# A graph network on one core: the prologue's work dealt out anew among VectorE, ScalarE and GpSimd

## What is computed

```python
def reference(x, adj, W1, b1, W2, b2, W):        # x 128x128x64, adj 128x128x128, about 12% of it > 0
    h = relu(layernorm(x))
    mask = (adj > 0)
    W1a, W1b = W1[:F], W1[F:]
    diff = h[:, :, None, :] - h[:, None, :, :]
    g = relu((h @ W1a)[:, :, None, :] + diff @ W1b + b1)
    x = x + einsum('bjkh,bjk->bjh', g, mask) @ W2 + mask.sum(-1)[..., None] * b2
    h = relu(layernorm(x))
    return x + einsum('bnm,bmf->bnf', adj, h) @ W.T
```

## Time and profile before

| | us |
|---|---|
| median of 3 runs | 849.71 |
| lowest, highest | 849.04, 850.85 |
| the profiled execution, its own time | 851.92 |
| its span in the trace | 849.9 |

### The profile page before, as it was taken

One profiled execution on the slowest core, in us unless ns is written; L12 is line 12 of the kernel. 1 busy time (PEld: TensorE's weight loads), 2 busy tenths in 40 slices (PEclk: granted clock), 3 DMA queues, 4 the chain that ended last, 5 costly groups with the idle time before them and its releaser, 6 DMA issues.

```text
span 849.9 us, 26682 instructions
## 1 busy us (share of the span) xinstructions
PE 809.7 (95%) x8242; PEld 712.0 (84%) x8243; DVE 820.1 (96%) x2908; ACT 794.5 (93%) x2241; POOL 610.8 (72%) x1164
## 2 busy tenths in 40 slices
PE   3779999999999999999999999999999999999996
PEld 1447888988898889888988898888888988998884
DVE  6989999999999999999999999999999999999994
ACT  4768999999999999999999999999999999999993
POOL 0855777777787777777777777777777777777773
PEclk9779999999999999999999999999999999999998
DMA  9800000000000000000000000000000000000000
GB/s 336 324 1 2 2 14 20 21 15 20 21 20 9 21 21 18 17 21 21 20 9 21 20 21 15 21 20 20 8 20 21 20 14 21 21 20 9 27 1 23
DMA packets 26704, 27.54 MB, mean 32 GB/s; under 512 B 3520, under 2 KB 24512, under 8 KB 25536
## 3 DMA queue, kind: packets, MB, share of 16 engines
q1 hardware_dynamic: 25488, 25.37, 8.8%
q10 hardware_dynamic: 1072, 0.43, 0.2%
HBM read 21.59 MB, written 4.19 MB: 30 GB/s over the span
## 4 chain that ended last, share of the span: by engine, by line
PE 84%; DVE 6%; issue 3%; ACT 3%; POOL 2%; DMA 1%; SPq 0%; ACTq 0%; POOLq 0%; DVEq 0%
PE ring L400 45%; PE ring L428 8%; PE prep L457 4%; DVE acc L804 4%; PE post L494 3%; PE post L500 3%; PE post L487 3%; PE post L488 3%; PE prep L465 3%; PE prep L468 2%; PE prep L463 2%; PE post L492 2%; POOL rstd L969 1%; DMA x_all<-x_nbf_dram 1%; PE prep L459 1%
## 5 line engine op out<-in xcount | busy, mean ns | idle before, releaser
L804 DVE SCALAR_TENSOR_TENSOR acc<-ring,acc 128x384 f32<-128x384 f32 x896 | 491.7, 549 | 0.6
L561 ACT COPY ring<-P 128x384 f32<-128x384 f32 x1024 | 467.5, 506 | 23.4 <-DVE acc L804 10.4
L400 PE MATMUL ring<-PQ,onehot_space 128*128 128x192 f16 x4096 | 418.7, 247 | 5.5 <-ACT ring L561 2.4
L400 PEld LDWEIGHTS ring<-PQ,onehot_space 128*128 128x128 f16 x4096 | 328.7, 99 | 42.7 <-issue 13.5
L900 POOL TENSOR_SCALAR start<-P,spare 128x192 f32<-128x192 f32 x128 | 131.9, 1030 | 135.5 <-ACT P L611 135.0
L924 POOL TENSOR_TENSOR row_space<-row_space 128x192 f32<-128x192 f32 x256 | 153.3, 599 | 29.7 <-ACT row_space L599 14.0
L790 DVE TENSOR_SCALAR onehot_space<-mask_all 128x512 f16<-128x512 f16 x512 | 161.8, 318 | 0.0
L428 PE MATMUL ring<-PQ,owner 128*128 128x384 f16 (+1 forms) x512 | 94.0, 306 | 0.0
L400 PE MATMUL ring<-PQ,onehot_row 128*128 128x192 f16 x768 | 84.4, 246 | 2.0 <-DVE onehot_row L852 2.0
L599 ACT ACTIVATE row_space<-ring 128x576 f32<-128x576 f32 x128 | 83.1, 649 | 0.7 <-PE ring L400 0.7
L804 DVE SCALAR_TENSOR_TENSOR acc<-ring,start 128x384 f32<-128x384 f32 x128 | 71.2, 556 | 6.8 <-PE ring L400 2.5
(11 more groups left out here) (138 smaller groups left out, 1422.0 us busy)
## 6 DMA issues: line engine op xcount, KB each, us to landing
onehot_space<-adj_kbj_dram SPq DMA_DIRECT2D x8, 1024.0 KB, 17.6
adj_again<-adj_kbj_dram SPq DMA_DIRECT2D x128, 64.0 KB, 2.0
x_all<-x_nbf_dram SPq DMA_DIRECT2D x8, 512.0 KB, 18.4
out_dram<-x_all SPq DMA_DIRECT2D x32, 128.0 KB, 1.9
consts<-consts_dram SPq DMA_DIRECT2D x1, 192.0 KB, 2.5
scratch<-w1a_dram ACTq DMA_DIRECT2D x2, 48.0 KB, 4.4
scratch<-w1b_dram ACTq DMA_DIRECT2D x2, 48.0 KB, 6.9
scratch<-b_dram ACTq DMA_DIRECT2D x1, 96.0 KB, 10.2
```

The source lines that it names most:

```text
L400: last = nc.tensor.matmul(to, hot(s), parts[:, part, H:2 * H], start=False, stop=(part == 1), skip_group_check=True)
L561: return nc.scalar.copy(slots[to][:, bank_], src.unsqueeze(1).broadcast_to([N, PER_BANK, H]))
L804: return nc.vector.scalar_tensor_tensor(sums, slots[to][:, bank_], 0.0, start[:, :, :] if first else sums, ALU.max, ALU.subtract if first ...
```

## The change

Nothing of the computation is altered. In the prologue:

- **SP**: the x loads of parts 4 to 7 move one place back, so that adjacency 5, 6 and 7 are each issued ahead of x 4, 5 and 6.
- **DVE**: `scale` is cut into pieces (`largest`, `largest_of_rows`, `scale`, `second_parts`) that stand between masks and statistics, in an order written out by hand. It loses the fold, the first parts, the copies within `w_parts`, the scaling of W2, the jk copies of part 7 and `spare`.
- **ACT** copies all codes, jk of part 7 too; the first four parts are written out, the last four loop. It makes the scaled first parts (new lines 654 and 655) behind part 2, and both early h1 behind part 3.
- **POOL** gets the fold (`folded`), the copies within `w_parts` (`parts_ready`), the scaling of W2 (`scaled`), and `spare` in four operations. The norm's fourth power moves behind the start values of graph 0 and step -1.
- **PE**: the second half of `codes(1)` stands behind the wait for the largest weight. Part 7 waits for `parts_ready` and `scaled` as it had for `weights_ready`.

```diff
@@ sync
             for g in range(PARTS):
-                b = slice(g * PER_PART, (g + 1) * PER_PART)
                 if g >= STAGES:
                     sp.wait_ge(mask_ready, g - STAGES + 1)
-                sp.dma_start(adj_stage[g % STAGES], adjT[:, b, :]).then_inc(adj_in[g], 16)
-                sp.dma_start(x_all[:, b, :], x[:, b, :]).then_inc(x_in[g], 16)
+                sp.dma_start(adj_stage[g % STAGES], adjT[:, g * PER_PART:(g + 1) * PER_PART, :]).then_inc(adj_in[g], 16)
+                if g < EARLY:
+                    x_part(g)
+                elif g > EARLY:
+                    x_part(g - 1)
+            x_part(PARTS - 1)
@@ tensor
             codes(0)
-            codes(1)
+            codes(1, range(QUADS // 2))
 
             pe.wait_ge(largest_ready, 1)
             nc.tensor.matmul(post[0:1, 0:N], to_scale[:, 0:1], ident, start=True,
                              stop=True).then_inc(largest_seen, 1)
+            codes(1, range(QUADS // 2, QUADS))
             pe.wait_ge(largest_ready, 2)
...
-            pe.wait_ge(weights_ready, 2)
+            pe.wait_ge(parts_ready, 1)
+            pe.wait_ge(scaled, 1)
@@ scalar
             codes(0)
-            with nc.scalar.Fori(1, LATE // 2) as g:
+            codes(1)
+            codes(2)
+            act.wait_ge(scale_ready, 1)
+            nc.scalar.activation(w_parts[:, 0, :, 0:H], w_pq[:, :].rearrange("p (k h) -> p k h", k=3), ACT.Copy,
+                                 scale=to_scale[:, 2:3]).then_inc(first_parts_ready, 1)
+            codes(3)
+            act.wait_ge(norm1_ready, 1)
+            lead(step, hi=-1)
+            with nc.scalar.Fori(EARLY, PARTS) as g:
                 codes(g)
-            act.wait_ge(norm1_ready, 1)
-            lead(step, hi=-2)
-            with nc.scalar.Fori(LATE // 2, LATE) as g:
-                codes(g)
-            lead(step, lo=-2, hi=-1)
-            codes(LATE)
             lead(step, lo=-1)
-            for g in range(LATE + 1, PARTS):
-                codes(g)
@@ vector, the order of the prologue
+            mask(0)
+            norm1_stats(0)
+            mask(1)
+            norm1_stats(1)
+            largest()
+            mask(2)
+            largest_of_rows()
+            moments(0)
+            norm1_stats(2)
+            scale()
+            mask(3)
+            norm1_stats(3)
+            moments(1)
+            mask(4)
+            second_parts()
+            mask(5)
+            norm1_stats(4)
+            mask(6)
+            norm1_stats(5)
+            moments(2)
+            mask(7)
+            norm1_stats(6)
+            norm1_stats(7)
+            moments(3)
...
-            chain(nc.vector.scalar_tensor_tensor(spare[:, :], owned, -float(ROW_SLOTS), deg[:, :], ALU.mult, ALU.add))
-            chain(nc.vector.scalar_tensor_tensor(spare[:, :], fits, float(SLOTS * LOOPED), spare[:, :], ALU.mult, ALU.add))
-            chain(nc.vector.tensor_scalar(spare[:, :], spare[:, :], -float(COVERED + SLOTS * LOOPED), -1.0, ALU.add, ALU.mult))
@@ gpsimd
+            pool.wait_ge(first_weights_in, 16 * 5)
+            nc.gpsimd.tensor_tensor(w_pq[:, 0:H], w_pq[:, 0:H], w1b, ALU.add)
+            nc.gpsimd.tensor_scalar(w_pq[:, H:2 * H], w1b, -1.0, None, ALU.mult).then_inc(folded, 1)
+            norm1(0)
+            norm1(1)
+            pool.wait_ge(second_parts_ready, 1)
+            nc.gpsimd.tensor_copy(w_parts[:, :, :, H:H + N], w_parts[:, :, :, 0:N]).then_inc(parts_copied, 1)
+            pool.wait_ge(parts_copied, 1)
+            nc.gpsimd.tensor_copy(w_parts[F:2 * F, 0, 2, :], w_parts[F:2 * F, 1, 2, :]).then_inc(parts_ready, 1)
+            pool.wait_ge(parts_ready, 1)
+            lead(step, hi=-1)
+            pool.wait_ge(weights_in, 16 * 6)
+            nc.gpsimd.tensor_scalar(w2a[:, :], w2a[:, :], to_scale[:, 3:4], None, ALU.mult)
+            nc.gpsimd.tensor_scalar(w2b[:, :, :], w2b[:, :, :], to_scale[:, 3:4], None, ALU.mult).then_inc(scaled, 1)
+            norm1(2)
+            pool.wait_ge(owned_ready, 1)
...
             some = load_any(nc.gpsimd)
             pool.wait_ge(tables_ready, 1)
             pool.wait_ge(p_ready, 1)
             start_sums(0, 0)
+            lead(step, lo=-1)
+            norm1(GROUPS - 1)
             graphs(nc.gpsimd, step, some)
```

More of the change, by code:

```diff
@@ L361, in _, with codes @@
         def _(pe):
-            def codes(g):
+            def codes(g, quads=range(QUADS)):
                 pe.wait_ge(mask_ready, g + 1)
-                for q in range(QUADS):
+                for q in quads:
                     quad = g * QUADS + q
@@ L725, in _, with norm1_stats, moments @@
             m_even, m_odd, s_even, s_odd = (stats1[:, :, k] for k in (1, 4, 2, 5))
[L726 to L729 removed]
+            def norm1_stats(g):
                 dve.wait_ge(x_in[g], 16)
                 for b in range(g * PER_PART, (g + 1) * PER_PART):
[L732 to L739 removed]
+                    last = nc.vector.bn_stats(stats1[:, b, :], x_all[:, b, :])
+                if g % GROUP == GROUP - 1:
+                    last.then_inc(stats1_ready, 1)
+            def moments(k):
+                dve.wait_ge(stats1_ready, k + 1)
+                b = slice(k * GROUP * PER_PART, (k + 1) * GROUP * PER_PART)
                 nc.vector.tensor_tensor(mom[:, 0, b], m_even[:, b], m_odd[:, b], ALU.add)
@@ L963, in step, with norm1 @@
                     nc.gpsimd.tensor_tensor(shift2[:, k, :], neg2[:, k, :], rstd2[:, k, :], ALU.mult).then_inc(norm2_ready, 1)
-            for g in range(GROUPS):
+            def norm1(g):
                 b = slice(g * GROUP * PER_PART, (g + 1) * GROUP * PER_PART)
```

84 lines of the change are left out of this document (34 added, 50 removed).

## The result

| | before | after |
|---|---|---|
| median, 5 runs each on one chip | 850.46 us (849.04 to 850.85) | 843.7 us (840.92 to 845.98) |
| ratio | | 0.9915, 95% interval 0.9899 to 0.9932 |
| the profiled execution, its own time | 851.92 | 845.98 |
| its span | 849.9 | 844.1 |

A forecast was written before the change was run, and what follows sets the result against it. The prediction took the end of code copying, with ACT's idle hole in the prologue, to set the loop's start and so the end. Terms -2.5, -0.9, -0.9 and +1.4 gave -2.9: 849.7 to 846.8 us, range 844.4 to 849.5.

The forecast's parts named there:

- The main loop should keep its pace: Main loop: the change touches nothing behind the prologue, so only the loop's start shifts and its length stays.
- the sign: Main loop: a length changed by more than half a microsecond would show the argument that the shift is all wrong.
- Term 1: Prologue, last code copy on ACT: ends at 47.0 us against 49.54, -2.5 us; with gaps vanishing, about 45.2.
- The covers: Prologue: DVE's masks, load order, POOL's fold and weights keep up with ACT, costed at nothing; fold done by 15.2.
- rival D: Prologue, POOL's fold: code loading at POOL's first call makes it 5.6 us late, 852.4 us; chance 0.08 with anything like it.
- POOL's two copies: Prologue, POOL's weights for part 7: copies of 768 and 320 elements take 4.2 us together, bounds 2.0 to 5.2.
- Terms 2 and 3: Prologue, DVE's chain to the first sum: three spare operations leave (-0.9 us), start values no longer wait for POOL's power (-0.9).
- Term 4: Loop start, graph 1: DVE waits for POOL's start values behind the fourth norm power, +1.4 us, bounds 0.9 to 1.9.
- The sum: Whole kernel: the four terms, -2.5 - 0.9 - 0.9 + 1.4, give -2.9 us.

The follow-up runs named there:

- the old place: Changed kernel with 15 one-element memsets ahead on DVE, so graph 0's first sum is instruction 249 as in the kernel before: 848.24 us, ratio 0.9966.
- the order alone: Kernel before with only the order of masks and weights' scaling changed (DVE, and PE's second half of code group 1): 848.79 us, ratio 0.9971.
- the early power: Changed kernel with POOL's fourth norm power put back behind the third, ahead of the loop's first start values: 845.04 us, ratio 0.9927.
- late ring writes: Changed kernel with PE's ring writes moved from ahead of the owner sums to behind them: 841.58 us (ratio 0.989), again 842.68 (0.9894).

## Why the prediction was wrong, step by step

**"The main loop should keep its pace": the step that failed.** It held for the work in the loop, and was false for its place. The prediction had named the sign itself: if the loop's own length changes by more than half a microsecond, the argument that the shift is all is wrong. It changed by 5.07. The change takes 15 entries out of DVE's list ahead of the loop, and with them four pauses out of the loop. Tried in both directions: with the old place the changed kernel is at 0.9966 (0.9954 to 0.9979) of the kernel before, which is 0.0034 x 850.62 (the kernel before in that batch) = **2.9 us** (2.4 by the medians), the number forecast for the prologue; without the pauses the kernel before is at 0.9956, 3.7 us (2.9 by the medians). So of the measured 6.8 us some 3 are the prologue's and 3 to 4 the place's, and what is left is within the spread of the pace. ACT's list lost 32 entries in the change, and no run moved its place alone; as DVE's place by itself brings the changed kernel's loop back to 763.99 us (the kernel before: 761.85 to 764.50), little is left for it.

Why an instruction whose number is 63 modulo 128 is late is not shown, but the traces say what happens there. The page of the profile has, in the kernel before and, but for the share, in the changed one (packets, MB, share of the 16 DMA engines' span):

```profile
q14 instruction: 76, 0.62, 0.2%
```

These are packets of 8 KB, one in 11 us. In all 18 traces each of DVE's 30 entries from number 319 on that are 63 modulo 128 has such a packet that starts between 0.54 us ahead of the entry and 1.05 us behind it. So DVE's list is fetched, as it looks, in blocks of 128 entries, and a fetch begins as DVE passes these places. That the fetch makes the sum late is argued from this coincidence; no run tried it. Nor is it settled why first sums pause most: at other entries with such numbers the idle time was at most 0.24 us, and mostly none.

**Term 1, -2.5: right in mechanism, mis-sized.** The last copy ended at 46.3, not 47.0: -3.2. Group 2 began at 20.51, 0.3 later than forecast; from there 25.8 us where I had 26.8: eight copies back to back took 3.8 (20.51 to 24.33), the first parts 0.68 (24.33 to the next copy at 25.01), and the gaps between groups mostly vanished, the lower bound that I had named. The version with the order alone had 2.0 of it.

**The covers held.** The fold was ready at 14.7 where I had 15.2 as the late bound, with its first call at 13.47 right behind the bias: rival D is refuted. It was POOL's first arithmetic, though not its first instruction: four memsets of constants stand at 0.24 to 0.43 us, in both kernels. By the rule of the Trainium skill (GPSIMD Engine Reference, 2.1 Instruction dispatch), about 6 us for the first call to a freshly loaded kernel, any loading must here have been over before 13.5 us; the trace shows none of it behind the call. The masks 3 to 7 started at 21.55, 25.84, 27.71, 30.88 and 35.21, each 0.5 to 0.7 ahead of forecast. POOL's two copies took 0.82 and 0.45 us where I had 4.2 for both: even the lower bound of 2.0 was too dear. I had taken slopes from rows with f32 operands and these are half-precision copies; that this is the reason no run shows.

**Terms 2 and 3, -1.8 together: they didn't arrive.** From the first count to the first sum took 10.21 us before and 10.58 after (10.16 and 10.28 in two more traces of the changed kernel), where I had 8.4. The wait for POOL went, as forecast. In its place came 0.46 (projection), 1.12 (owner sums) and 0.81 of slower one-hots (3.53 against 2.72). I had taken DVE's chain to be serial on DVE's own work. Three spare operations of 0.9 us had covered PE's owner sums; when they left, PE with its ring writes ahead was late next. The prediction put PE's part in this chain at nothing, without a reason. `spare` back on DVE shows it: graph 0 at 56.84, against 56.5 to 56.9 in the three traces of the changed kernel. "Where a stall goes, say what is late next" was done for POOL and not for PE. With the ring writes behind the sums the wait was still 0.76:

```profile
50.97 0.28 DVE L802 TENSOR_SCALAR loops<-ring 1x128 int32<-1x128 f32 x1 [0.76 <-PE ring L542]
```

That is from the second run of that version; there the two sums themselves, begun when DVE's `owned` is ready, are what DVE waits for.

TensorE's clock has a share in this wait that I had overlooked. In all six traces with the old end of the prologue the four ring writes ran at the full clock in 1.03 us; in eleven of the twelve others they ran at half of it in 1.91. In the twelfth, the changed kernel with 12 memsets on DVE, the clock was back at full from 50.5 us on, and DVE's wait for the sums was 0.45 in place of 1.12, with the same wait of 0.46 for the projection ahead of it:

```profile
50.77 0.38 PE L544 MATMUL ring<-scratch 128*128 128x128 f32 x2
51.42 0.28 DVE L807 TENSOR_SCALAR loops<-ring 1x128 int32<-1x128 f32 x1 [0.45 <-PE ring L545]
```

In the changed kernel PE stands idle for 1.73 us ahead of the first projection (0.86 before), and the clock is at half behind that. So some 0.7 of the 1.12 us go with the clock, by this one trace.

**Term 4, +1.4: zero in this trace.** The power began at 55.45 and took 5.54, the start values 0.95: ready at 62.26 where I had 62.1 to 63.1. That was right; but DVE came at 62.45 in place of 61.2, since terms 2 and 3 had not arrived. In the second trace of the changed kernel DVE came at 62.0 and did wait, 0.28 us, for POOL's start values; in the third these were 0.7 ahead of it. The kernel with the early power had no gain in its time.

**The sum, -2.9**, was met at graph 0 (-2.94) and graph 1 (-3.08) by errors that cancel, which is luck: 0.7 too little gain in term 1, 2.2 too much in terms 2 and 3, 1.4 too much cost in term 4.

**The tail**, which the prediction didn't speak of, takes 19.8 to 20.7 us in eight of the 18 traces and 21.4 to 22.2 in ten, and which one isn't the kernel's doing: late ring writes had 20.19 once and 21.85 once. It goes with the granted clock, which is at half for the last 4.9 to 7.4 us in the eight and for the last 11.8 to 13.7 in the ten. Windows of after and of the first run with late ring writes; columns are the window, its length, busy time of the engines, the clock, DMA:

```profile
830.00:844.00 14.00, 8.01 (x31) 6.11 (x29) 1.75 (x8) 2.62 (x8) 2.15 (x6) 0.53 0.08 25
```

```profile
829.00:839.00 10.00, 4.19 (x21) 2.86 (x19) 1.75 (x8) 1.80 (x6) 1.32 (x4) 0.74 0.10 33
```

The clock is at half for nearly the whole of the last 14 us in the one and for half of the last 10 in the other. The 2.40 us that the profiled execution lost there are no effect of the change.

## What to carry to other kernels

An edit ahead of a long unrolled loop also moves the loop within its engine's instruction list, and here that moved the time about as much as the edit did: before crediting or blaming a change for what happens in code that it doesn't touch, look whether single iterations are slow at fixed numbers, and shift the list by a few idle instructions in both kernels. When work leaves a serial chain, ask of every semaphore that the chain passes what its releaser does in the meantime, and at which clock, not only of the wait that is visible before. And a forecast that is met can be met by errors that cancel; only the waits in the trace after tell.

## What the runs showed of the hardware

- Two one-element memsets at the head of VectorE's list made an 850 us kernel 2.9 us faster (ratio 0.9956, 0.9939 to 0.9972). Pauses of 0.25 to 0.47 us stood at first sums whose number in the list is 63 modulo 128, in the 11 cases within the loop that the count named for the three kernels built to have them, and at no first sum of graphs 8 to 124 of the kernels for which it named none.
- At each of VectorE's entries with such a number, from 319 on, an 8 KB packet of the queue of kind "instruction" started within 0.54 us ahead and 1.05 us behind, in all 18 traces.
- Such a pause costs 0.7 to 1.2 us of the time. In the graphs at and behind it, work on VectorE takes longer, as it seems for running beside GpSimd's work in another way: three `onehot_row` took 0.88 us where 0.38 to 0.57 is usual, `from_first` 0.58 where 0.21 to 0.35 is.
- 13 one-hots took 2.71 to 2.72 us while GpSimd was in a power and 3.42 to 3.60 us while it made start values, PQ and parts.
- Four multiplies of 128x512 took 1.03 us at the full granted clock and 1.91 at half.
- GpSimd's half-precision copy took 0.82 us for 128x768 and 0.45 for 64x320, 1.1 ns per element of the first. Its first arithmetic of the program, 0.59 us for 128x192 at 13.47 us, showed no time for preparation.
